# One comparison over a whole quad in place of four, in the second message stage of a graph network kernel

## The reference, cut to what matters

```
msgs   = x1[src]                                   # 106250 rows of 256
agg    = segment_sum(msgs, dst, 6250)
counts = segment_sum(ones, dst, 6250)
agg    = agg / max(counts, 1)
x2     = layernorm(x1 + relu(agg @ W.T + b))
```

## Time and profile before

| what | value |
|---|---|
| median of 3 runs | 4305.1 us (4304.66 to 4308.48) |
| span of the profiled execution | 4476.8 us, 78542 instructions |
| the same execution's own time | only its span is given; 171.7 us over the median |
| busy share of the span | PE 73%, PEld 53%, DVE 61%, ACT 32%, POOL 67% |
| chain that ended last, by line | line 843 10%, line 846 4%, line 1510 1%, line 1497 1% |

### The profile page before, as it was taken

One profiled execution on the slowest core, in us unless ns is written; L12 is line 12 of the kernel. 1 busy time (PEld: TensorE's weight loads), 2 busy tenths in 40 slices (PEclk: granted clock), 3 DMA queues, 4 the chain that ended last, 5 costly groups with the idle time before them and its releaser, 6 DMA issues. The chain is left out here.

```text
span 4476.8 us, 78542 instructions
## 1 busy us (share of the span) xinstructions
PE 3279.6 (73%) x16047; PEld 2393.6 (53%) x16048; DVE 2711.5 (61%) x11910; ACT 1448.7 (32%) x2712; POOL 3017.8 (67%) x2631
## 2 busy tenths in 40 slices
PE   7557777777787777777777778795666666666675
PEld 3246666665666666666666667584343434443344
DVE  6356666676666666666666668677444444444454
ACT  2224444444444444444444445531000000000004
POOL 0258888888888888888888887612666666666634
PEclk9778899898889888889989899997777777777788
DMA  4655555555555555555555555754333333333313
GB/s 147 214 154 94 93 93 94 94 93 93 94 94 94 92 93 94 93 94 93 93 94 93 93 93 82 144 162 132 91 90 91 90 90 91 91 90 90 91 51 116
DMA packets 336077, 455.15 MB, mean 102 GB/s; under 512 B 53568, under 2 KB 282524, under 8 KB 335772
## 3 DMA queue, kind: packets, MB, share of 16 engines
q0 software_dynamic: 199680, 327.32, 39.1%
q1 hardware_dynamic: 116844, 105.48, 8.1%
q10 hardware_dynamic: 19248, 19.66, 1.3%
HBM read 296.41 MB, written 155.62 MB: 101 GB/s over the span
## 5 line engine op out<-in xcount | busy, mean ns | idle before, releaser
L557 POOL DMA_INDIRECT sum<-arena,sidx x832 | 1323.3, 1591 | 293.5 <-issue 245.8
L546 POOL DMA_INDIRECT arena<-p_tab,esrc x832 | 818.0, 983 | 457.0 <-issue 418.6
L587 POOL DMA_INDIRECT arena<-x_tab,esrc x832 | 794.6, 955 | 460.0 <-issue 182.8
L843 PE MATMUL ps<-arena 128*125 x1760 | 714.3, 496 | 435.6 <-issue 237.5
L709 PE MATMUL ps<-arena 128*128 128x256 f32 x1664 | 570.6, 503 | 419.9 <-ACT arena L954 419.2
L746 PE MATMUL ps<-w,arena 128*128 128x256 f32 x3328 | 833.6, 383 | 3.9 <-ACT arena L964 3.9
L843 PEld LDWEIGHTS ps<-arena 128*125 128x125 f32 x1760 | 402.2, 244 | 733.0 <-issue 663.1
L1510 DVE TENSOR_TENSOR arena<-ps,arena 125x257 f32 x880 | 374.8, 426 | 635.9 <-remote 208.2
L709 PEld LDWEIGHTS ps<-arena 128*128 128x128 f32 x1664 | 398.5, 251 | 528.4 <-issue 460.2
L746 PEld LDWEIGHTS ps<-w,arena 128*128 128x128 f32 x3328 | 567.4, 190 | 121.2 <-issue 4.9
L1309 DVE TENSOR_TENSOR arena<-ps,arena 128x256 f32 x880 | 373.1, 424 | 411.7 <-issue 224.2
(11 more groups left out here) (182 smaller groups left out, 3953.6 us busy)
## 6 DMA issues: line engine op xcount, KB each, us to landing
arena<-loc_tab SPq DMA_DIRECT2D x220, 125.0 KB
arena<-sum SPq DMA_DIRECT2D x200, 128.0 KB, 2.1
sum<-scr ACTq DMA_DIRECT2D x3, 6400.0 KB
arena<-p_tab,esrc POOLq DMA_INDIRECT x832
sum<-arena,sidx POOLq DMA_INDIRECT x832
arena<-x_tab,esrc POOLq DMA_INDIRECT x832
sum<-scr SPq DMA_DIRECT2D x1, 6400.0 KB
arena<-x_tab SPq DMA_DIRECT2D x50, 128.0 KB, 2.0
```

Source lines behind the costliest of these rows:

```text
L546: pool.indirect_dma_start(out=ring0[:, tile % RING, :], out_offset=None, in_=p_tab[:, :], in_offset=bass.IndirectOffsetOnAxis(ap=esrc[:, t ...
L557: pool.indirect_dma_start(out=sums[u][:, :], in_=tot[:, par, u, :], in_offset=None, out_offset=bass.IndirectOffsetOnAxis(ap=sidx[:, par, u ...
L587: pool.indirect_dma_start(out=ring[:, tile % RING, 0:D], out_offset=None, in_=x1_tab[:, :], in_offset=bass.IndirectOffsetOnAxis(ap=esrc[:, ...
L843: nc.tensor.matmul(ps[0:NB, u, 0:CW], same1[:, par, u, :], ring[:, bass.ds(at[u], 1), :].rearrange("p a c -> p (a c)"), start=True, stop=T ...
```

## The change

The four comparisons of 125 columns of a quad become one comparison of 500 columns. The node row is repeated over the four visits, and the column of each visit over its 125 nodes; both inputs are now tensors with a step of zero in one dimension. The result has the same layout and the semaphore `hot` is raised by that one instruction. Nothing else changes.

```
-                for u in range(QT):
-                    last = nc.vector.tensor_scalar(same1[:, par, u, :], nodes[:, :], vloc[:, bass.ds(q * QT + u, 1)],
-                                                   None, ALU.is_equal)
-                last.then_inc(s["hot"], 1)
+                nc.vector.tensor_tensor(same1[:, par, :, :], nodes[:, :].unsqueeze(1).to_broadcast([P, QT, NB]),
+                                        vloc[:, bass.ds(q * QT, QT)].unsqueeze(2).to_broadcast([P, QT, NB]),
+                                        ALU.is_equal).then_inc(s["hot"], 1)
```

## The result

| | median us | runs |
|---|---|---|
| before | 4305.2 | 4304.7 to 4308.5 (4 runs) |
| after | 4336.6 | 4335.0 to 4338.8 (4 runs) |

The ratio is 1.0074, 95% interval 1.0062 to 1.0086: the change costs 31 us. The profiled execution of after has a span of 4333.3 us, close to its runs; that of before had 4476.8. So the two spans can't be set against each other, and I come back to that where the kernel before is profiled again.

The account below looks back on a forecast made before the run. POOL's own pace was taken to bound the gathering stage, DVE the drain. From 4305.1 us, 4.3 gained in the drain, 35.4 lost to held gathers and 1.7 coming back gave 4334.5 us, range 4262 to 4380.

Parts of the forecast that it names:

- Pauses of the profile: While POOL gathers: 155 us of pauses, mostly of the profiled execution and not of timed runs; held at 7 in 10.
- POOL's pace as the bound: While POOL gathers: 1.258 us a gather, about 1047 us for 832, bounds timed runs; PE and DVE have slack.
- Length of the comparison: The new DVE comparison of 500 columns takes 0.67 us, by 0.98 ns a column.
- Drain: DVE after the last gather: 0.33 us gained a quad, 4.3 us over 13 quads (2.5 to 6.1).
- The lock: DVE comparison with two SBUF inputs holds a gather's early part for 0.59 us; POOL cannot make it up.
- The size of the loss: While POOL gathers: 0.17 us lost a comparison, 35.4 us over 208 quads (0 to 112).
- what goes: The four old comparisons also touch the gathers a little; at most 1.7 us comes back.
- first moment: A gather wants to go on 0.05 us after its start; being held there costs 0.14 us a comparison on average.
- second moment: A second such point in a gather, some 0.13 us later, adds 0.05 us a comparison.
- no meeting on the port: Rival: comparisons fall late in gathers or hold only briefly, so only the drain gains; 4299 to 4303 us, chance 0.20.
- DVE with PE as the bound: Rival: pauses are real in timed runs and POOL has slack, so fewer DVE instructions give 4264 us; chance 0.25.
- The case in which each comparison hits: Upper bound of the port case: every comparison holds a gather, 112 us lost, 4411 us; taken as its tail.

Follow-up runs that it names:

- PSUM experiment: The kernel after, with the comparison's node row read as f32 from a PSUM bank, so only one input is in SBUF: 4301.2 us, ratio 0.9995.
- the other place: The kernel after, with the comparison call moved behind the first addition of the quad in DVE's order: 4315.9 us, ratio 1.0025.

## Why the prediction was right

Predicted were 4334.5 us, measured 4336.6. By its steps:

- **Pauses of the profile, POOL's pace as the bound: right.** Shown by the second profile of before (idle time 253 us and not 408), and by twice the one-input comparisons, which left POOL's idle time at 253 us. What caused the pauses of the first one stays open; nothing was run on it. The trace says where they sit, in DVE's own queue: while POOL gathers, 251 register and semaphore instructions of DVE take over 0.4 us each there, 176 us in sum, and at most one does in the second profile (line 1497's reach 1385 ns in the earlier trace rows and 82 there).
- **Length of the comparison: right.** 0.67 us said, 670 ns measured.
- **Drain: right in mechanism, slightly over in sum.** 0.33 us a quad said, 0.36 measured. The sum of 13 quads was put at 4.3 us; from the last gather to the last addition it is 3.3 us (47.3 against 44.0).
- **The lock: right that a long comparison over a gather's start prolongs it, wrong on where.** The prediction's 0.59 us from the comparison's start less 0.05 us into the gather is 0.54, and lead and prolongation sum to 0.54. But it let a comparison cost the gather even when it starts up to 0.05 us behind the gather's start; the border is 0.035 us ahead of that start. The PSUM experiment shows that this comparison holds no gather once its row lies in PSUM; that only an instruction of two tensors can hold one is refuted by the short comparisons of before. Whether a one-input comparison of 500 columns would hold a gather as long was not tried. The lock given by the page "SBUF — State Buffer" of the Trainium skill ("SBUF: two separate sides") agrees in kind. What the trace adds is that a comparison which starts behind the gather's start leaves it at 949 to 962 ns, even while it stands over the rest of it.
- **The size of the loss: right by luck, by three errors that cancel.** I said 0.17 us a comparison, 35.4 us, or 33.7 with what goes. Measured: 33.6 us on the stretch; 37.4 us of gather time over 953 ns against 3.4 in before. But my 0.17 was a first moment in random phase (0.14) and part of a second moment 0.13 us later (0.05). The first is too large: with the border at 0.035 us it is 0.505 x 0.505 / 2 / 1.258 = 0.10 us, 21 us in all. The second does not exist for line 587: comparisons that start 0.05 to 0.20 us behind a gather's start (31 of them) leave it at 949 to 962 ns. What makes both up is that the phases are not random: 111 of 206 comparisons start in the harmful place, where equal chance would put 83, and 67 of them in 0.15 us of its costly end (1.05 to 1.20 us after one gather's start), where equal chance would put 25. What the pair of instructions in the earlier trace rows met in the first message stage stays open.
- **What goes: 1.7 us said at most.** The gathers of before had 3.4 us over 953 ns in the second profile, 0.6 with PSUM; so the four comparisons cost about 3 us.
- **Two readings of the rows were wrong, without weight in the sum.** In the earlier trace rows the 3.95 us of idle time end at 3486.02, so DVE was busy until 3482.07: a third comparison started at 3481.78. And in the earlier trace rows 1.14 us and four additions at 0.64 us would be 3.70 us; the next comparison starts 0.34 us after the fourth addition's start, which makes the 3.39.

Of the rivals, no meeting on the port (0.20) and DVE with PE as the bound (0.25) both fell: the former by the timeline of after, the latter by the doubled one-input comparisons. The case in which each comparison hits fell by the count, 111 of 206.

## What to carry to other kernels

When POOL's own pace bounds a stage, price every change of DVE by what it keeps POOL from, not by what DVE saves: here 0.36 us saved per quad on an engine with slack went with 0.16 us lost on the one without. Four short instructions can beat one long one, if another engine has to get in between; and where a long one is wanted, one of its two inputs in PSUM lets the other engine pass. Before a sum is laid on a profile, set its span against the timed runs: 172 us were in the one and not in the other, and the idle time before the bounding engine said where.

## What the runs showed of the hardware that was not expected

- Who comes first at a gather's start holds the other. A comparison of 0.67 us with a lead of over 0.035 us prolongs the gather, by 0.50 us at most. One that starts from 0.032 us ahead of the gather's start to 0.036 us behind it costs the gather nothing and is held itself: it takes 676 to 743 ns and ends 0.71 us after the gather's start. With the row in PSUM the four comparisons with a lead under 0.033 us take 668 to 679 ns.
- Late in a gather, the one-input comparisons are held. Line 1497 in the second profile of before:

```profile
L1497 DVE TENSOR_SCALAR arena<-nodes,vloc x880: 207/278/518, 3080.9 to 4183.4; 128x125 f32<-128x125 bf16 x176
```

  In both traces of before, those that start 0.50 to 0.65 us after a gather's start end 0.99 to 1.00 us after it, when the gather is just done, and the longest, from 0.47 us, takes 522 ns; most others take some 280. The two-input comparisons have no such tail there: 669 to 680 ns in after, and 290 at most where there are four of them. Why the one kind is held late in a gather and the other only at its start was not tried.
- DVE's phase against POOL's is not random here, and moves with the order of DVE's instructions: at the other place, 151 of 207 comparisons start in the first 0.70 us of a gather, where they cost it nothing, and 88 of 206 do in after. How much the phase varies from run to run isn't shown: the ten runs of that kernel spread by 13 us, but so do, by 12 us, the eleven runs of the kernel with its row in PSUM, whose gathers are not prolonged at all.
